# A down projection in split fp32r instead of plain fp32, in a kernel of a recurrent block and a gated FFN

## The chip, the core and the metric

The kernel runs on one core of a Trainium2 chip. A core has a matrix engine (TensorE, PE here; PEld is its weight load), a vector engine (VectorE, DVE), a scalar engine (ScalarE, ACT), GpSimd (POOL) and SyncE (SP), which run their own queues of instructions in order and wait for each other on semaphores. The metric is the device time of one launch in microseconds (us), the median of several runs.

## The reference, cut to what matters

```python
def fp4_quant_dequant(x):                 # blocks of 16 along the last dim
    xb = x.reshape(shape[:-1] + (shape[-1] // BLOCK, BLOCK))
    scale = jnp.maximum(jnp.max(jnp.abs(xb), axis=-1, keepdims=True) / 6.0, 1e-12)
    xn = xb / scale
    return (_GRID[jnp.searchsorted(_MID, jnp.abs(xn))] * jnp.sign(xn) * scale).reshape(shape)

def fp4_linear(x, w):
    return jnp.einsum('bsk,nk->bsn', fp4_quant_dequant(x), fp4_quant_dequant(w))

# x: (16, 512, 256); w_gate, w_up: (704, 256); w_down: (256, 704)
xn = _layernorm(x)
s = recurrent_block(xn)                   # rmsnorm, causal conv, pointwise; minGRU; FFN 256-1024-256
h = silu(fp4_linear(xn, w_gate)) * fp4_linear(xn, w_up)
g = silu(fp4_linear(h, w_down))           # the down projection
out = x + s * g
```

## The kernel before

The 16 sequences are 16 chunks of 512 tokens; a chunk is T = 4 tiles of 128 tokens. A prologue loads and quantises the weights; then `body(c)` runs once for each chunk: chunk 0 and chunk 15 stand alone, chunks 1 to 14 are seven rounds of a loop of two bodies. Each engine has its own list, written out by hand, and there is no scheduler: what stands in the list is the order.

**One chunk on PE.** `gate_up(c, t, h)` makes the gate and up products of tile t, half h (352 of 704 columns), in fp32r: both operands are held as a high part and a remainder, and `product` (L811) issues three products, high by high, high by low, low by high. Among the gate_up groups stand `sum_squares` and `spread_scale` (the rms norm), then come `gru`, `ff2` of the chunk before and `ff1`. The quantised hidden rows (`hq`) of tile t are transposed on PE by `hq_transposes` into banks 2 and 3 of `w_ps` (six tiles of 128 columns), ACT copies them into `hq_t` (`hq_columns`, L693), and `down` (L882) multiplies them by `dn`. The down projection of a chunk is spread out: tile 0 stands at the end of its own body (`hq_transposes(c, 0)`, the transposes of `xq`, `down(c, 0)`, then `pointwise(c + 1)`), tiles 1, 2 and 3 stand in the next chunk's body among its gate_up, gru and ff2.

**Plain fp32.** `hq_t` and `dn` are fp32. `down` runs over six tiles of the 704 hidden columns, of which the sixth has only `LAST` = 64 rows. In the trace each such matmul is two records, so a down tile is 12.

```python
for k in range(KI):
    rows = P if k < KI - 1 else LAST
    last = product(bank[:, 0:D], hq_t[0:rows, k, :], dn[0:rows, k, :], k == 0, k == KI - 1)
```

**One chunk on DVE.** DVE does the quantising of the hidden rows (`hidden_scales`, `fp4_ratios`, `fp4_round`, `hidden_values`), the product of silu and up (`hidden(c, t, h)`, L455), the norms (`add_squares`, `clamp_sums`, `scaled`, `scaled_low`), the scan (`recurrence`), the outputs and the front of the next chunk: `front_moments`, `front_rows`, `front_fp4` (quantises the 512 by 256 inputs, L391 writes `xq`), `front_taps` (the convolution, L443 and L446 write `y`, which `pointwise` reads) and `front_fp4_low` (L452 writes `xq_lo`, which `gate_up(c + 1, 0, 0)` waits for). At the end of a body DVE starts on tile 1's rows (`hidden_scales(c, 1)`), and the next body begins with their rounding and with `conv_residual`, which makes `x1`.

**Waits that matter.** `gate_up(c, t, h)` for t over 0 waits until `hidden` has read the bank of two groups before (`hid_ready`); `hidden` waits for ACT's silu, which waits for PE. `hq_transposes` waits for `hq_ready` from DVE. `sum_squares` waits for `sqs_ready`; in the second half of a chunk it hangs on `recurrence` and the squares on ACT.

Of the kernel before, what the change touches and what calls it, by code (L numbers as in the profile page):

```python
# [19 lines left out]
F32 = mybir.dt.float32  # L20
# [37 lines left out]
def mixed_recurrent_kernel(nc, x, columns, pw_t, gru_t, w1_t, w2_t, w_gate, w_up, w_down, identity, out):  # L58
# [15 lines left out]
    with ctx:  # L74
# [6 lines left out]
        def sem(name):  # L81
# [19 lines left out]
        gu_lo = sb("gu_lo", [P, KD, 2 * NI], F32R)  # L101
        dn = sb("dn", [P, KI, D])

# [17 lines left out]
        x1 = sb("x1", [P, KD, L])  # L121
        sq = sb("sq", [P, KD, L])
        sqs = sb("sqs", [P, L])
        ss_row = sb("ss_row", [P, T])
        inv_rms = sb("inv_rms", [P, T])
        xs = sb("xs", [P, KD, L])
        xs_hi = sb("xs_hi", [P, KD, L], F32R)
        xs_lo = sb("xs_lo", [P, KD, L], F32R)
# [9 lines left out]
        hq = sb("hq", [P, 2, KI * P])  # L138
        hq_t = sb("hq_t", [P, KI, P])
        q_amax = sb("q_amax", [P, 64])  # L140
# [24 lines left out]
            sem(n) for n in ("const_loaded", "gu_loaded", "dn_loaded", "pw_loaded", "gru_loaded",  # L165
                             "w1_loaded", "w2_loaded"))
        constants_ready = sem("constants_ready")
        small_ready = sem("small_ready")
        wscaled = sem("wscaled")
# [5 lines left out]
        wqlo_ready = sem("wqlo_ready")  # L175
        dnt_ready = sem("dnt_ready")
        stats_ready = sem("stats_ready")
# [42 lines left out]
        hqt_done = sem("hqt_done")  # L220
        hqt_ready = sem("hqt_ready")
        dn_done = sem("dn_done")
# [11 lines left out]
        def ff1_bank(j):  # L234

            return gu_ps[:, 1 - j // 2 % 2, j % 2, :]

        def weight_places(p, dst):
# [110 lines left out]
        def _(dve):  # L349
# [116 lines left out]
            def hidden_values(c, t, rounded):  # L466
                dve.wait_ge(hqt_done, KD + T * c + t - 1)
                fp4_values(hq[:, t % 2, 0:NI], NBI, rounded).then_inc(hq_ready, 1)

            def add_squares(n):  # L470

                dve.wait_ge(sq_ready, KD * (n + 1))
                V.tensor_tensor(sqs[:], sq[:, 0, :], sq[:, 1, :], ALU.add).then_inc(sqs_ready, 1)
# [26 lines left out]

            def recurrence(c):

                for k in range(KD):
                    dve.wait_ge(sigh_ready, KD * c + k + 1)
                    V.scalar_tensor_tensor(cand[:, k, :], gu_ps[:, k, 1, :], 0.5, cand[:, k, :],
                                           ALU.add, ALU.max).then_inc(cand_ready, 1)
                    dve.wait_ge(cand_ready, KD * c + k + 1)
                    s = steps.mark(V.tensor_tensor(cand[:, k, :], cand[:, k, :], take[:, k, :], ALU.mult))
                    dve.wait_ge(dve_step, s)
                    s = steps.mark(V.tensor_tensor_scan(x2[:, k, :], keep[:, k, :], cand[:, k, :], 0.0,  # L510
                                                        ALU.mult, ALU.add))
                    dve.wait_ge(dve_step, s)
                    V.tensor_tensor(x2[:, k, :], x2[:, k, :], x1[:, k, :], ALU.add).then_inc(x2_ready, 1)

# [40 lines left out]
            def down_weight(e):  # L555

                dve.wait_ge(wqt_done, NFULL + e)
                quantise(dn_rows[:, e, :], hq[:, e, 0:NI], NBI).then_inc(wq_ready, 1)


            prologue_steps = steps.n
# [4 lines left out]
            def body(c, parity, tail, front):  # L566
# [24 lines left out]
                if tail:  # L591
                    ratios = fp4_ratios(hid[:, 3, :], NBI, scales)
                else:
                    down_weight(1)
                scaled(c * 2, x1, w_ps[:, 1, :])
                if tail:
                    dve.wait_ge(dve_step, ratios)
# [5 lines left out]
                if tail:  # L603
                    hidden_values(c - 1, 3, rounded)
                if front:
                    front_moments(c + 1)
                recurrence(c)
                add_squares(c * 2 + 1)
# [15 lines left out]
                if front:  # L624
                    front_fp4(c + 1)
                    front_taps(c + 1)
                ratios = fp4_ratios(hid[:, 1, :], NBI, hidden_scales(c, 1))
# [6 lines left out]
            for t in range(1, T):  # L634
                if t > 1:
                    ratios = fp4_ratios(hid[:, t, :], NBI, hidden_scales(B - 1, t))
                hidden_values(B - 1, t, fp4_round(NBI, ratios))
            for t in range(T):
                dve.wait_ge(g_ready, T * (B - 1) + t + 1)
                output(B - 1, t, gu_ps[:, t // 2, t % 2, :])  # L640
                dve.wait_ge(sg_ready, T * (B - 1) + t + 1)
                if t == 0:
                    dve.wait_ge(xres_ready, B)
                V.tensor_tensor(o[:, t, :], o[:, t, :], x_res[:, 1, t, :], ALU.add).then_inc(last_ready, 1)
# [3 lines left out]
        def _(act):  # L648
# [24 lines left out]
            def squares(n, ready, c, src):  # L673
                for k in range(KD):
                    act.wait_ge(ready, KD * c + k + 1)
                    act.wait_ge(sqs_ready, n)
                    A.activation(sq[:, k, :], src[:, k, :], ACT.Square).then_inc(sq_ready, 1)

# [14 lines left out]
            def hq_columns(c, t):  # L693
                act.wait_ge(hqt_done, KD + T * c + t + 1)
                act.wait_ge(dn_done, T * c + t)
                A.copy(hq_t[:], w_ps[:, 2:4, :].rearrange("p b n -> p (b n)")[:, 0:KI * P]
                       .rearrange("p (k n) -> p k n", n=P)).then_inc(hqt_ready, 1)

# [56 lines left out]
            def down_columns(e):  # L755
                act.wait_ge(hqt_done, e + 1)
                A.copy(dn[:, :, e * P:(e + 1) * P],
                       w_ps[:, 2:4, :].rearrange("p b n -> p (b n)")[:, 0:KI * P]
                       .rearrange("p (k n) -> p k n", n=P)).then_inc(dnt_ready, 1)

# [47 lines left out]
        def _(pe):  # L808
# [73 lines left out]
            def down(c, t, bank=w_ps[:, 2, :]):  # L882
                pe.wait_ge(hqt_ready, T * c + t + 1)
                for k in range(KI):
                    rows = P if k < KI - 1 else LAST
                    last = product(bank[:, 0:D], hq_t[0:rows, k, :], dn[0:rows, k, :], k == 0, k == KI - 1)
                last.then_inc(dn_done, 1)
# [70 lines left out]
            def down_weight(e):  # L958

                pe.wait_ge(wq_ready, NFULL + 2 + e)  # L960
                pe.wait_ge(dnt_ready, e)
                for k in range(KI):
# [4 lines left out]
            def body(c, parity, tail, front):  # L967
# [32 lines left out]
                if tail:  # L1000
                    ff2(c - 1, 2, w_ps[:, 2, :], (g_ready, T * c))
                    ff2(c - 1, 3, w_ps[:, 3, :], (hqt_ready, T * c))
                ff1(c, range(KF // 2))
                if not tail:
                    pe.wait_ge(dnt_ready, KD)
                if front:
# [65 lines left out]
```

## Time and profile before

| | |
|---|---|
| time, median of 3 runs | 1215.48 us (1215.27 to 1216.74) |
| span of the profiled execution | 1213.5 us |
| PE busy | 1150.5 us (95%) |
| PEld busy | 969.2 us (80%) |
| DVE busy | 1006.4 us (83%) |
| ACT busy | 531.6 us (44%) |
| chain that ended last | PE 92%, DVE 6% |
| down matmuls, 768 records in the trace | 191.5 us busy |

Times in the rows are counted from the start of the span. A timeline row gives start, duration, engine, line, operation, what is written from what, the shape, and in brackets the idle time of the engine before it with what ended that. Matmul records overlap, because PE is pipelined: what a matmul costs is the distance from its start to the next one's start, not its own duration. From about 115 us on every chunk repeats the one before after 70.5 us.

### The profile page before, as it was taken

To read this page: it belongs to the slowest core of one execution; us is meant where nothing else is said; L and a number is where in the kernel's file an instruction comes from. 1 tells how busy PE (TensorE), PEld (TensorE's weight loads), DVE (VectorE), ACT (ScalarE), POOL (GpSimd) and SP (SyncE) were. 2 spreads that over 40 slices of the span, in tenths; PEclk is the share of its full clock that TensorE was granted. 3 is DMA by queue.
4 is the path that set the end of the run, shared out by engine and by line. 5 is a ranking of instruction groups with operands and counts; after the bars stand their busy time and mean duration, and the time that the engine had idled before them with its cause. 6 is when DMAs were issued, how large, how long until landed. Compare 5 with 4: busy or idle time off the path is not lost.

```text
span 1213.5 us, 17503 instructions
## 1 busy us (share of the span) xinstructions
PE 1150.5 (95%) x5922; PEld 969.2 (80%) x5922; DVE 1006.4 (83%) x1844; ACT 531.6 (44%) x839; POOL 144.0 (12%) x122
## 2 busy tenths in 40 slices
PE   3276999999999999999999999999999999999998
PEld 2274888888888887888888798888878888887887
DVE  7868788897978889797888989798897979889783
ACT  4134435453444545444454544445454444545441
POOL 3000010100201020020102011020101102010010
PEclk8587999999999999999999999999999999999999
DMA  6000001000000100000010000001000000100000
GB/s 204 0 1 1 18 1 35 1 19 17 18 18 0 35 0 19 16 18 18 0 35 0 32 4 17 18 0 35 0 35 0 18 18 0 35 0 18 1 18 18
DMA packets 20883, 22.42 MB, mean 18 GB/s; under 512 B 864, under 2 KB 20064, under 8 KB 20832
## 3 DMA queue, kind: packets, MB, share of 16 engines
q1 hardware_dynamic: 20000, 21.04, 5.2%
q10 hardware_dynamic: 832, 0.87, 0.2%
q14 instruction: 39, 0.32, 0.1%
q8 instruction: 12, 0.20, 0.1%
HBM read 13.51 MB, written 8.39 MB: 18 GB/s over the span
## 4 chain that ended last, share of the span: by engine, by line
PE 92%; DVE 6%; issue 0%; ACT 0%; DMA 0%; POOL 0%; ACTq 0%; DVEq 0%; POOLq 0%
PE gu_ps L818 44%; PE w_ps L818 37%; PE w_ps L878 3%; PE w_ps L825 2%; PE gu_ps L861 1%; PE w_ps L924 1%; PE gu_ps L825 1%; PE w_ps L861 1%; DVE q_y L385 1%; DVE q_y L387 1%; DVE q_y L372 1%; DVE q_amax L362 1%; PE gu_ps L870 1%; PE w_ps L870 1%; DVE hq L391 0%
## 5 line engine op out<-in xcount | busy, mean ns | idle before, releaser
L818 PE MATMUL w_ps<-w,act 128*128 128x256 f32 x960 | 217.1, 379 | 0.0
L818 PEld LDWEIGHTS w_ps<-w,act 128*128 128x128 f32 x960 | 177.7, 190 | 21.7
L818 PE MATMUL w_ps<-dn,hq_t 128*128 128x256 f32 (+1 forms) x768 | 191.5, 391 | 0.2
L818 PE MATMUL gu_ps<-gu_hi,xq_hi 128*128 128x352 f32 x512 | 179.0, 350 | 1.0 <-DVE gu_lo L518 1.0
L818 PEld LDWEIGHTS w_ps<-dn,hq_t 128*128 128x128 f32 (+1 forms) x768 | 137.5, 189 | 39.2 <-issue 21.2
L818 PE MATMUL gu_ps<-gu_lo,xq_hi 128*128 128x352 f32 x512 | 167.4, 327 | 0.0
L818 PE MATMUL gu_ps<-gu_hi,xq_lo 128*128 128x352 f32 x512 | 166.6, 325 | 0.0
L458 DVE TENSOR_TENSOR hid<-sl,gu_ps 128x352 f32<-128x352 f32 x128 | 65.6, 513 | 108.0 <-ACT sl L685 107.9
L685 ACT ACTIVATE sl<-gu_ps 128x352 f32<-128x352 f32 x128 | 59.4, 464 | 194.2 <-PE gu_ps L818 193.6
L322 POOL TENSOR_TENSOR inv_rms<-ss_row,neg_half 128x4 f32<-128x4 f32 x32 | 40.5, 1267 | 594.2 <-DVE ss_row L478 594.2
L818 PE MATMUL gu_ps<-xs_hi,w_hi 128*128 128x512 f32 x256 | 106.2, 415 | 4.1 <-DVE xs_lo L491 4.1
L724 ACT ACTIVATE act<-gu_ps,cols 128x512 f32<-128x512 f32 x128 | 86.6, 689 | 53.3 <-PE gu_ps L818 53.1
L818 PEld LDWEIGHTS gu_ps<-gu_hi,xq_hi 128*128 128x128 f32 x512 | 97.7, 191 | 15.0 <-issue 8.6
L818 PE MATMUL gu_ps<-xs_hi,w_lo 128*128 128x512 f32 x256 | 102.8, 401 | 0.0
L818 PE MATMUL gu_ps<-xs_lo,w_hi 128*128 128x512 f32 x256 | 102.3, 400 | 0.0
L818 PEld LDWEIGHTS gu_ps<-gu_lo,xq_hi 128*128 128x128 f32 x512 | 97.8, 191 | 3.6 <-issue 3.6
L818 PEld LDWEIGHTS gu_ps<-gu_hi,xq_lo 128*128 128x128 f32 x512 | 97.5, 190 | 0.0
L691 ACT CAST xs_hi<-xs 128x512 fp32r<-128x512 f32 x64 | 37.8, 617 | 108.7 <-DVE xs L485 108.7
L385 DVE TENSOR_TENSOR q_y<-q_y,q_m 128x704 f32<-128x704 f32 (+3 forms) x88 | 82.4, 937 | 3.0
L387 DVE TENSOR_TENSOR q_y<-q_y,q_m 128x704 f32<-128x704 f32 (+3 forms) x88 | 82.4, 936 | 3.0
L703 ACT ACTIVATE g<-w_ps 128x256 f32<-128x256 f32 x64 | 24.6, 384 | 100.1 <-PE w_ps L818 99.9
L391 DVE TENSOR_TENSOR hq<-q_y,q_scale 128x704 f32<-128x704 f32 (+1 forms) x72 | 62.6, 869 | 1.9
(112 smaller groups left out, 2045.8 us busy)
## 6 DMA issues: line engine op xcount, KB each, us to landing
x_in<-x_dram SPq DMA_DIRECT2D x16, 512.0 KB, 3.5
out_dram<-o SPq DMA_DIRECT2D x15, 512.0 KB, 2.9
act<-w_t_dram SPq DMA_DIRECT2D x1, 1024.0 KB, 11.4
w<-w_t_dram SPq DMA_DIRECT2D x1, 1024.0 KB, 13.9
act<-w_down_dram SPq DMA_DIRECT2D x1, 704.0 KB, 9.5
hid<-w_gate_dram SPq DMA_DIRECT2D x1, 640.0 KB, 5.6
hid<-w_up_dram SPq DMA_DIRECT2D x1, 640.0 KB, 8.7
keep<-gru_t_dram ACTq DMA_DIRECT2D x1, 512.0 KB, 8.0
```

Of the source, the lines that this page charges most:

```text
L322: nc.gpsimd.tensor_tensor(inv_rms[:], ss_row[:], neg_half[:], ALU.pow).then_inc(inv_ready, 1)
L385: s = steps.mark(V.tensor_tensor(yv, yv, mv, ALU.add))
L387: return steps.mark(V.tensor_tensor(yv, yv, mv, ALU.subtract))
L391: return V.tensor_tensor(blocks(dst, nb), blocks(q_y[:, 0:nb * FP4_BLOCK], nb), spread(q_scale[:, 0:nb], nb), ALU.mult)
L458: V.tensor_tensor(hid[:, t, h * HALF:(h + 1) * HALF], sl[:, h, :], gu_ps[:, h, 1, 0:HALF], ALU.mult).then_inc(hid_ready, 1)
L685: A.activation(sl[:, h, :], gu_ps[:, h, 0, 0:HALF], ACT.Silu).then_inc(silu_ready, 1)
L691: A.copy(xs_hi[:, k, :], xs[:, k, :]).then_inc(xshi_ready, 1)
L703: A.activation(g[:, t, :], bank[:, 0:D], ACT.Silu).then_inc(g_ready, 1)
L724: A.activation(act1[:, j, :], ff1_bank(j), ACT.Gelu, bias=b1c[:, j:j + 1]).then_inc(gelu_ready, 1)
L818: done = M.matmul(psum, l, r, start=first and i == 0, stop=last and i == len(terms) - 1)
L825: last = M.transpose(bank[:, t * P:(t + 1) * P], src[:, t, k * P:(k + 1) * P], ident[:])
L878: last = M.transpose(w_ps[:, 2 + k // 4, k % 4 * P:(k % 4 + 1) * P], hq[:, t % 2, k * P:(k + 1) * P], ident[:])
```

## The change

- `dn` becomes `dn_hi` and `dn_lo`, `hq_t` becomes `hqt_hi` and `hqt_lo`, all fp32r. ACT's copy writes the high part; a new DVE instruction subtracts it from what stands in PSUM and writes the remainder: `hidden_low` for the rows, `down_weight_low` for the two halves of the weights, in chunk 0.
- `down` waits for both parts and issues three fp32r products for each of six full tiles (the last 64 columns of `hq` are zero): 18 matmuls instead of six fp32 ones.
- `hidden_low(c - 1, t)` for t = 1, 2, 3 and `hidden_low(c, 0)` are put into DVE's list; `recurrence` is cut into its two halves so that `hidden_low(c - 1, 3)` stands between them.
- `sq`, the buffer of the squares, becomes the same memory as `xs`, with a wait for `xslo_ready` ahead of the squares.

The diff, cut:

```diff
+        sq = xs
...
+            def hidden_low(c, t):
+
+                dve.wait_ge(hqthi_ready, T * c + t + 1)
+                dve.wait_ge(dn_done, T * c + t)
+                V.tensor_tensor(hqt_lo[:], hqt_ps, hqt_hi[:].bitcast(F32), ALU.subtract).then_inc(hqtlo_ready, 1)
...
                 add_squares(c * 2)
+                if tail:
+                    hidden_low(c - 1, 1)
                 hidden(c, 1, 1)
...
+                    down_weight_low(0)
                     down_weight(1)
                 scaled(c * 2, x1, w_ps[:, 1, :])
+                if tail:
+                    hidden_low(c - 1, 2)
...
-                recurrence(c)
+                recurrence(c, 0)
+                if tail:
+                    hidden_low(c - 1, 3)
+                recurrence(c, 1)
...
                 if front:
                     front_fp4(c + 1)
+                hidden_low(c, 0)
+                if front:
                     front_taps(c + 1)
...
                 hidden_values(B - 1, t, fp4_round(NBI, ratios))
+                hidden_low(B - 1, t)
...
                     act.wait_ge(sqs_ready, n)
+                    act.wait_ge(xslo_ready, KD * n)
...
-                A.copy(hq_t[:], w_ps[:, 2:4, :].rearrange("p b n -> p (b n)")[:, 0:KI * P]
-                       .rearrange("p (k n) -> p k n", n=P)).then_inc(hqt_ready, 1)
+                A.copy(hqt_hi[:], hqt_ps).then_inc(hqthi_ready, 1)
...
-                pe.wait_ge(hqt_ready, T * c + t + 1)
+                pe.wait_ge(hqthi_ready, T * c + t + 1)
+                pe.wait_ge(hqtlo_ready, T * c + t + 1)
                 for k in range(KI):
-                    rows = P if k < KI - 1 else LAST
-                    last = product(bank[:, 0:D], hq_t[0:rows, k, :], dn[0:rows, k, :], k == 0, k == KI - 1)
+                    last = product(bank[:, 0:D], (hqt_hi[:, k, :], hqt_lo[:, k, :]),
+                                   (dn_hi[:, k, :], dn_lo[:, k, :]), k == 0, k == KI - 1)
```

Where the new instruction stands in DVE's list. First the end of a body, shown for chunk 0, before (`xq` is the last write of `front_fp4`, `y` that of `front_taps`, `q_amax<-hid` begins the scales of tile 1):

```order
L387 TENSOR_TENSOR q_y<-q_y,q_m 128x1024
L391 TENSOR_TENSOR xq<-q_y,q_scale 128x1024
L443 SCALAR_TENSOR_TENSOR y<-w_ps,cols,y 128x511
L446 SCALAR_TENSOR_TENSOR y<-w_ps,cols,y 128x510
L443 SCALAR_TENSOR_TENSOR y<-w_ps,cols,y 128x511
L446 SCALAR_TENSOR_TENSOR y<-w_ps,cols,y 128x510
L362 TENSOR_REDUCE q_amax<-hid 128x44
```

The same place on DVE after the change:

```order
L394 TENSOR_TENSOR q_y<-q_y,q_m 128x1024
L398 TENSOR_TENSOR xq<-q_y,q_scale 128x1024
L481 TENSOR_TENSOR hqt_lo<-w_ps,hqt_hi 128x768
L450 SCALAR_TENSOR_TENSOR y<-w_ps,cols,y 128x511
L453 SCALAR_TENSOR_TENSOR y<-w_ps,cols,y 128x510
L450 SCALAR_TENSOR_TENSOR y<-w_ps,cols,y 128x511
L453 SCALAR_TENSOR_TENSOR y<-w_ps,cols,y 128x510
L369 TENSOR_REDUCE q_amax<-hid 128x44
```

The remainder of tile 0 now stands ahead of the four instructions of the convolution; all behind it keeps its order. Second, DVE's list around `scaled` in the first half of a body, before (`xs` from `w_ps` is `scaled`, the first `hid` is `hidden(c, 2, 1)`, the second `hidden(c, 3, 0)`):

```order
L458 TENSOR_TENSOR hid<-sl,gu_ps 128x352
L372 TENSOR_TENSOR q_y<-hid,q_inv 128x704
L485 TENSOR_TENSOR xs<-w_ps,x 128x512 x2
L458 TENSOR_TENSOR hid<-sl,gu_ps 128x352
L491 TENSOR_TENSOR xs_lo<-xs,xs_hi 128x512 x2
```

The same place after:

```order
L465 TENSOR_TENSOR hid<-sl,gu_ps 128x352
L379 TENSOR_TENSOR q_y<-hid,q_inv 128x704
L498 TENSOR_TENSOR xs<-w_ps,x 128x512 x2
L481 TENSOR_TENSOR hqt_lo<-w_ps,hqt_hi 128x768
L465 TENSOR_TENSOR hid<-sl,gu_ps 128x352
L504 TENSOR_TENSOR xs_lo<-xs,xs_hi 128x512 x2
```

The remainder of tile 2, for which PE's `down(c - 1, 2)` waits, stands behind `scaled`; nothing else is moved.

## Rows read from the trace of the kernel before

**Rows 1.** The page, busy us, share of the span and instructions of each engine:

```profile
PE 1150.5 (95%) x5922; PEld 969.2 (80%) x5922; DVE 1006.4 (83%) x1844; ACT 531.6 (44%) x839; POOL 144.0 (12%) x122
```

**Rows 2.** Windows, one chunk: length, busy us of PE, PEld, DVE, ACT, POOL, clock, DMA:

```profile
620.12:690.62 70.50, 70.48 (x368) 59.55 (x368) 60.00 (x110) 32.39 (x52) 8.82 (x7) 1.00 0.05 15
```

**Rows 3.** Timeline of PE in that chunk: gate_up(c,1,0), down of tiles 1 and 2, sum_squares:

```profile
631.08 0.40 PE L818 MATMUL gu_ps<-gu_hi,xq_hi 128*128 128x352 f32 x1
...
635.88 3.03 PE L818 MATMUL w_ps<-dn,hq_t 128*128 128x256 f32 x12
638.84 0.43 PE L818 MATMUL gu_ps<-gu_hi,xq_hi 128*128 128x352 f32 x1
...
645.83 2.95 PE L818 MATMUL w_ps<-dn,hq_t 128*128 128x256 f32 x12
...
663.54 1.05 PE L861 MATMUL gu_ps<-ones,sqs 128*128 128x1 f32 x8
```

**Rows 4.** Timeline of PE: 3rd and 24th product of an ff1 and a gate_up group:

```profile
613.28 0.40 PE L818 MATMUL gu_ps<-xs_hi,w_lo 128*128 128x512 f32 x1
...
618.19 0.39 PE L818 MATMUL gu_ps<-xs_hi,w_lo 128*128 128x512 f32 x1
...
626.97 0.32 PE L818 MATMUL gu_ps<-gu_hi,xq_lo 128*128 128x352 f32 x1
...
630.35 0.32 PE L818 MATMUL gu_ps<-gu_hi,xq_lo 128*128 128x352 f32 x1
```

**Rows 5.** Groups of instructions by line and shape, whole span: count, busy us, mean ns:

```profile
L458 DVE TENSOR_TENSOR hid<-sl,gu_ps 128x352 f32<-128x352 f32 x128 | 65.6, 513 | 108.0 <-ACT sl L685 107.9
...
L452 DVE TENSOR_TENSOR xq_lo<-gu_ps,xq_hi 128x512 fp32r<-128x512 f32 x32 | 20.5, 683 | 0.1
```

**Rows 6.** Timeline of DVE: hidden(c,1,1), scaled, hidden(c,3,0), second half of recurrence:

```profile
635.72 0.52 DVE L458 TENSOR_TENSOR hid<-sl,gu_ps 128x352 f32<-128x352 f32 x1 [0.82 <-ACT sl L685]
...
645.46 1.28 DVE L485 TENSOR_TENSOR xs<-w_ps,x 128x512 f32<-128x512 f32 x2
647.78 0.52 DVE L458 TENSOR_TENSOR hid<-sl,gu_ps 128x352 f32<-128x352 f32 x1 [1.05 <-ACT sl L685]
...
658.64 0.68 DVE L505 SCALAR_TENSOR_TENSOR cand<-gu_ps,cand 128x512 f32<-128x512 f32 x1
```

**Rows 7.** Timeline of ACT: the copies of tiles 2, 3 and 0:

```profile
644.10 0.80 ACT L696 COPY hq_t<-w_ps 128x768 f32<-128x768 f32 x1 [0.62 <-PE w_ps L878]
...
657.19 0.80 ACT L696 COPY hq_t<-w_ps 128x768 f32<-128x768 f32 x1
...
689.77 0.80 ACT L696 COPY hq_t<-w_ps 128x768 f32<-128x768 f32 x1
```

**Rows 8.** Timeline of DVE: conv_residual, hidden(c,0,0) of this chunk; first of front_taps:

```profile
625.92 0.75 DVE L498 SCALAR_TENSOR_TENSOR x<-w_ps,cols,xn_t 128x512 f32<-128x512 f32 x1
...
629.34 0.52 DVE L458 TENSOR_TENSOR hid<-sl,gu_ps 128x352 f32<-128x352 f32 x1 [1.75 <-ACT sl L685]
...
686.34 0.74 DVE L443 SCALAR_TENSOR_TENSOR y<-w_ps,cols,y 128x511 f32<-128x511 f32 x1
```

**Rows 9.** Timelines of DVE and ACT in chunk 0, the quantising of w_down:

```profile
76.72 0.88 DVE L362 TENSOR_REDUCE q_amax<-act 128x44 f32<-128x704 f32 x1
...
82.85 1.28 DVE L485 TENSOR_TENSOR xs<-w_ps,x 128x512 f32<-128x512 f32 x2
...
78.99 0.80 ACT L757 COPY dn<-w_ps 128x768 f32<-128x768 f32 x1 [5.01 <-PE w_ps L963]
```

**Rows 10.** PE's wait in chunk 0 (timeline), and the window behind it:

```profile
87.00 0.47 PE L818 MATMUL gu_ps<-xs_hi,gru_hi 128*128 128x512 f32 x1 [2.50 <-DVE xs_lo L491]
...
88.00:91.30 3.30, 3.30 (x9) 2.54 (x8) 1.27 (x9) 1.09 (x2) 1.64 (x4) 0.50 0.00 0
```

**Rows 11.** Timelines at the end: ACT's copy of tile 0, PE's last down:

```profile
1181.51 0.80 ACT L696 COPY hq_t<-w_ps 128x768 f32<-128x768 f32 x1
...
1207.12 2.95 PE L818 MATMUL w_ps<-dn,hq_t 128*128 128x256 f32 x12
```

More of the change, by code:

```diff
@@ L101, in mixed_recurrent_kernel @@
         gu_lo = sb("gu_lo", [P, KD, 2 * NI], F32R)
-        dn = sb("dn", [P, KI, D])
+        dn_hi = sb("dn_hi", [P, KI, D], F32R)
+        dn_lo = sb("dn_lo", [P, KI, D], F32R)
         x_in = sb("x_in", [P, T, D])
@@ L121, in mixed_recurrent_kernel @@
         x1 = sb("x1", [P, KD, L])
-        sq = sb("sq", [P, KD, L])
         sqs = sb("sqs", [P, L])
@@ L138, in mixed_recurrent_kernel @@
         hq = sb("hq", [P, 2, KI * P])
-        hq_t = sb("hq_t", [P, KI, P])
+        hqt_hi = sb("hqt_hi", [P, KI, P], F32R)
+        hqt_lo = sb("hqt_lo", [P, KI, P], F32R)
         q_amax = sb("q_amax", [P, 64])
@@ L166, in mixed_recurrent_kernel @@
                              "w1_loaded", "w2_loaded"))
+        small_ready = sem("small_ready")
         constants_ready = sem("constants_ready")
-        small_ready = sem("small_ready")
         wscaled = sem("wscaled")
@@ L175, in mixed_recurrent_kernel @@
         wqlo_ready = sem("wqlo_ready")
-        dnt_ready = sem("dnt_ready")
+        dnhi_ready = sem("dnhi_ready")
+        dnlo_ready = sem("dnlo_ready")
         stats_ready = sem("stats_ready")
@@ L220, in mixed_recurrent_kernel @@
         hqt_done = sem("hqt_done")
-        hqt_ready = sem("hqt_ready")
+        hqthi_ready = sem("hqthi_ready")
+        hqtlo_ready = sem("hqtlo_ready")
         dn_done = sem("dn_done")
@@ L236, in ff1_bank @@
             return gu_ps[:, 1 - j // 2 % 2, j % 2, :]
+        hqt_ps = (w_ps[:, 2:4, :].rearrange("p b n -> p (b n)")[:, 0:KI * P]
+                  .rearrange("p (k n) -> p k n", n=P))
         def weight_places(p, dst):
@@ L499, in conv_residual, with recurrence @@
                                            ALU.add, ALU.add).then_inc(x1_ready, 1)
[L501 to L513, printed above, removed]
+            def recurrence(c, k):
+                dve.wait_ge(sigh_ready, KD * c + k + 1)
+                V.scalar_tensor_tensor(cand[:, k, :], gu_ps[:, k, 1, :], 0.5, cand[:, k, :],
+                                       ALU.add, ALU.max).then_inc(cand_ready, 1)
+                dve.wait_ge(cand_ready, KD * c + k + 1)
+                s = steps.mark(V.tensor_tensor(cand[:, k, :], cand[:, k, :], take[:, k, :], ALU.mult))
+                dve.wait_ge(dve_step, s)
+                s = steps.mark(V.tensor_tensor_scan(x2[:, k, :], keep[:, k, :], cand[:, k, :], 0.0,
+                                                    ALU.mult, ALU.add))
+                dve.wait_ge(dve_step, s)
+                V.tensor_tensor(x2[:, k, :], x2[:, k, :], x1[:, k, :], ALU.add).then_inc(x2_ready, 1)
             def weight_low(p):
@@ L558, in down_weight, with down_weight_low @@
                 quantise(dn_rows[:, e, :], hq[:, e, 0:NI], NBI).then_inc(wq_ready, 1)
+            def down_weight_low(e):
+                dve.wait_ge(dnhi_ready, e + 1)
+                cut = slice(e * P, (e + 1) * P)
+                V.tensor_tensor(dn_lo[:, :, cut], hqt_ps, dn_hi[:, :, cut].bitcast(F32),
+                                ALU.subtract).then_inc(dnlo_ready, 1)
             prologue_steps = steps.n
@@ L604, in body @@
                     hidden_values(c - 1, 3, rounded)
+                else:
+                    down_weight_low(1)
                 if front:
                     front_moments(c + 1)
-                recurrence(c)
+                recurrence(c, 0)
+                if tail:
+                    hidden_low(c - 1, 3)
+                recurrence(c, 1)
                 add_squares(c * 2 + 1)
@@ L756, in down_columns @@
                 act.wait_ge(hqt_done, e + 1)
-                A.copy(dn[:, :, e * P:(e + 1) * P],
-                       w_ps[:, 2:4, :].rearrange("p b n -> p (b n)")[:, 0:KI * P]
-                       .rearrange("p (k n) -> p k n", n=P)).then_inc(dnt_ready, 1)
+                A.copy(dn_hi[:, :, e * P:(e + 1) * P], hqt_ps).then_inc(dnhi_ready, 1)
             def body(c, parity, tail, front):
@@ L960, in down_weight @@
                 pe.wait_ge(wq_ready, NFULL + 2 + e)
-                pe.wait_ge(dnt_ready, e)
+                pe.wait_ge(dnlo_ready, e)
                 for k in range(KI):
@@ L1001, in body @@
                     ff2(c - 1, 2, w_ps[:, 2, :], (g_ready, T * c))
-                    ff2(c - 1, 3, w_ps[:, 3, :], (hqt_ready, T * c))
+                    ff2(c - 1, 3, w_ps[:, 3, :], (hqtlo_ready, T * c))
                 ff1(c, range(KF // 2))
                 if not tail:
-                    pe.wait_ge(dnt_ready, KD)
+                    pe.wait_ge(dnlo_ready, KD)
                 if front:
@@ L1025, in _ @@
             for t in range(1, T):
-                hq_transposes(B - 1, t, (hqt_ready, T * (B - 1) + t))
+                hq_transposes(B - 1, t, (hqtlo_ready, T * (B - 1) + t))
                 ff2(B - 1, t, gu_ps[:, t // 2, t % 2, :], None)
```

## The prediction

> **What bounds the kernel now.** I read the busy shares first: PE is busy 95% of the span, DVE 83% [rows 1]. Then one steady chunk by windows: from one down product of tile 0 to the next it takes 70.50 us, PE is busy for 70.48 of them at a granted clock of 1.00 (the 2.4 GHz level), DVE for 60.0 [rows 2]. So PE never waits in the loop, DVE has 10.5 us to spare, and a cheaper PE would be worth its saving if nothing took its place. Shares don't say that; places do. So I read, in order of time, where each of DVE's four new instructions (below: A for tile 1, B for tile 2, C for tile 3, D for tile 0) would stand: what DVE does there, when ACT's copy has ended, when PE wants the down product [rows 3, 6, 7, 8]. DVE works its queue in order, so an instruction that waits holds all behind it.
>
> **The price of the product.** Before, a down tile takes 638.84 - 635.88 = 2.96 us [rows 3]. After it is 18 products of 256 columns. The trace has fp32r products of 352 columns every (630.35 - 626.97)/21 = 0.161 us and of 512 columns every (618.19 - 613.28)/21 = 0.234 us [rows 4]: 0.456 ns a column either way. At that rate 256 columns take 0.117; a line with a fixed part, 512/2.4 and 352/2.4 taken off, gives up to 0.125; pure columns at 2.4 GHz 0.107. I take 0.117 (the two rows agree on it), so 18 x 0.117 = 2.10 us, **0.86 us less** per tile, and keep 0.107 to 0.125 for the range. The Trainium skill (TensorE: Matmul & The Clock Gate, Back-to-back issue gap) gives columns/2.4 + 2.5 ns, 109 ns here, and so 1.97 us a tile; by it 352 columns would take 149 ns where the row has 161, so the row decides. By the page the sum below would be some 4 us lower.
>
> **The price of the low part.** DVE's subtraction of 768 columns, one operand in PSUM, is not in the trace; its nearest rows are 352 columns in 513 ns and 512 columns, fp32r out, in 683 ns [rows 5]. Along that line 768 take 955 ns, and the next instruction starts some 0.87 after it. Bounds 0.90 and 1.00. It needs ACT's copy, 0.80 us [rows 7], which I leave as it is. Four of them are 3.8 us a chunk: less than DVE's spare 10.5 us, so the place of each decides. Now the walk, in times of the trace, through one chunk of the changed kernel. I add 0.04 to 0.1 us for a signal from engine to engine, as the rows show it.
>
> *A.* DVE stood idle for 0.82 us before hidden(c,1,1) at 635.72 [rows 6]; A fits in there (634.83 to 635.78), and PE wants the product at 635.88 [rows 3]. Nothing is lost, and all that follows comes 0.86 earlier.
>
> *B.* It stands behind scaled(), which began at 645.46 [rows 6], now 644.60, and lasts 1.20. So B runs from 645.8 to 646.76; ACT's copy (644.10 + 0.80 - 0.86 = 644.04) is long done [rows 7]. PE wants the product at 645.83 - 0.86 = 644.97 [rows 3] and gets it at 646.84: **a stall of 1.9 us**. It ends at 648.94, where the row puts 645.83 + 2.87 = 648.70: 0.24 late instead of 1.7 early. hidden(c,3,0) keeps its -0.86, since B lies in the 1.05 us for which DVE waited there [rows 6].
>
> *C.* Moved 0.24 by PE, ACT's copy runs 657.43 to 658.23 [rows 7]; DVE would be free at about 658.2. C takes 658.28 to 659.23, and recurrence(c,1), at 658.64 before [rows 6], starts at 659.15, 0.51 later. Squares, their sum and PE's sum_squares hang on it: 663.54 [rows 3] becomes 664.04. PE, done with its product at 663.0, stalls 1.0 us. Up to here a chunk has **lost 0.5**, not gained 3.
>
> *D.* From sum_squares to the transposes of tile 0 PE has no down product; that stretch is only moved by 0.5. ACT's copy runs 690.27 to 691.07 [rows 7]. DVE is done with front_fp4 where front_taps began, 686.34 + 0.5 [rows 8], and now stands for **4.2 us**, with front_taps, the scales of tile 1, xq_lo, the rounding of tile 1 and conv_residual queued behind the wait. D runs 691.10 to 692.05 and front_taps starts at 691.97, 5.6 later than before. From front_taps to conv_residual the rows have 625.92 - (686.34 - 70.5) = 10.08 us without a gap [rows 8], then 1.34 for its two instructions: hidden(c+1,0,0) starts at 691.97 + 10.08 + 1.34 = 703.39, not at 629.34 + 70.5 = 699.84, where DVE had waited 1.75 for it [rows 8]. On PE, down D starts at 692.13 and ends at 694.23; pointwise waits for y until 695.0; gate_up(0,0) for xq_lo until 698.6; then gate_up(1,0) for hidden(0,0), until 703.39 + 0.52 + 0.08 = 703.99. Before it began at 631.08 + 0.08 (the last transpose still ran) + 70.5 = 701.66 [rows 3]. **So a chunk takes 2.33 us more**, 72.8 instead of 70.5: 0.5 in its first half, 1.8 in the second. From there ACT and DVE again wait for PE (DVE by 0.8 us), so the next chunk begins in the same phase and the loss repeats.
>
> The rest of the edits. sq sharing xs makes the squares wait for xs_lo, which DVE made more than 10 us earlier (after 647.78, against 658.64 [rows 6]): nothing; without that cover it would cost the squares' start. The zero rows of the sixth tile are in the 18 products already.
>
> **Ends.** In chunk 0 down_weight_low(0) stands where the quantising of the second half of w_down began, 76.72 [rows 9], and needs ACT's copy, 78.99 + 0.80 [rows 9]; so that begins at 80.7, and as DVE is then the engine waited for (PE idle 2.50 at 87.00 [rows 10]), +4.0. D of chunk 0 adds 1.8. In the last chunk the first half adds 0.5; then D holds the quantising of tiles 1 to 3, done before under ff1, until ACT's copy, 1181.51 + 0.5 + 0.80 [rows 11]. It starts at 1183.7; each tile then goes round in quantising (82.85 - 76.72 = 6.1 to 6.3, from chunk 0 [rows 9]), transposes and copy 1.8, low part 0.9: 9.0. The last down product starts at 1183.7 + 6.3 + 2 x 9.0 + 4.4 (transposes and ff2 ahead of it) = 1212.4, not 1207.12 [rows 11], and is 0.86 shorter: +4.4 with the 0.5.
>
> **Sum.** 14 chunk periods x 2.33 = 32.6; chunk 0: 4.0 + 1.8; end: 4.4; together **+42.8 us**. The profiled span is 1213.5, the median 1215.48, 2.0 above it: 1213.5 + 42.8 + 2.0 = **1258 us**, 3.5% slower. Bounds: 36 products on the path of a chunk (down A and B) at 0.107 to 0.125, -5 to +4; three low parts at 0.90 to 1.00, 2 either way; ten signals by 0.05 each, 7 either way; chunk 0 and the end -2 to +7, mostly for the clock. As the price of this case: 1245 to 1275.
>
> **Rivals.**
> *Faster: the low parts vanish in DVE's spare time and PE alone decides.* For it: 70.48 of 70.50 us and DVE's 10.5 [rows 2]. Then 64 tiles x 0.86 = 55 us come off: 1160. It decides at D: ACT's copy would have to end by 686.3 for DVE to run through; it ends 4 us later, behind ff1. Between this and the forecast lies no change, if some 2.3 us of D's wait cost nothing: 1213 to 1218.
> *The clock falls.* In this trace PE stood idle for 2.50 us at 87.00, and 88.0 to 91.3 was granted 0.50, the 1.2 GHz level [rows 10]; the loop, without idle time, had 1.00 [rows 2]. My stalls are 1.9, 1.0, 1.0, 0.8, 0.2 and 0.8 us. If one a chunk took the clock down for such a stretch, PE would lose some 1.7 of 3.3 us: 14 x 1.7 = 24, so 1282, and twice that for two. It decides between idle times of 1.9 and 2.5 us. The Trainium skill (TensorE: Matmul & The Clock Gate, A second HAM failure mode: psum-queue depth-cycling) tells of a kernel in which brief idling of PE between groups of matmuls makes the clock swing between its two levels; by that rule this is the case to fear.
> *It doesn't do what it says: an fp32r product of 256 columns is no cheaper than half a plain fp32 one.* Then 18 x 0.216 (2.96 us less the half tile's edges, by 12) = 3.9 a tile; A and B carry 1.8 more each, 14 x 3.6 = 50: about 1310. Against it, the even 0.456 ns of 352 and 512 columns.
>
> **How the numbers follow.** Forecast 0.79, faster 0.07, no change 0.04, clock 0.06, no cheaper product 0.04. The forecast's own range, 1245 to 1275, holds perhaps nine tenths of its case; 1236 to 1290 takes in nearly all of it and half of the clock's: eight in ten. Within 0.2% (2.4 us, about what a measurement of this kernel can tell from no change) is 0.04; faster 0.07; slower 0.89.
>
> **What would show it.** In the profile after: down tiles of about 2.1 us; PE idle some 5.7 us a chunk, by the names of the low part (at B), sqs, y, xq_lo and hid; DVE idle before each low part of tile 0 for about 4.2 us, on ACT's copy; a period near 72.8; quantising strung out behind ff1 at the end. Wrong would be: no DVE wait at D (then the rivals hold), a half clock inside the loop, or products far from 0.117 us.

## The result, and the profile after

The changed kernel takes **1282.0 us** (median of 4 runs, 1280.8 to 1282.7) against 1216.1 of the kernel before, run beside it (1215.3 to 1217.5): a ratio of 1.055, 95% interval 1.053 to 1.056. Slower, as forecast, and inside the wide range (1236 to 1290), but 24 us above the point of 1258 and outside the forecast's own range (1245 to 1275). The profiled span is 1280.5 us, 67.0 above that of before. Three lines of its page: busy time, the queue q8, which brings blocks of instructions (packets, MB, share), and the chain that ended last:

```profile
PE 1126.8 (88%) x6306; PEld 980.0 (77%) x6306; DVE 1060.8 (83%) x1910; ACT 531.8 (42%) x839; POOL 144.1 (11%) x122
...
q8 instruction: 67, 1.10, 0.4%
...
PE 58%; DVE 29%; issue 8%; ACT 4%; DVEq 1%; DMA 0%; POOL 0%; ACTq 0%; POOLq 0%
```

PE does 24 us less than in [rows 1] and is no longer the only bound: a chain that was 92% PE is now 58%, with DVE at 29% and 8% "issue", which is an engine that waits for nothing the profile shows. The prices, from the groups of the whole span:

```profile
L848 PE MATMUL w_ps<-dn_hi,hqt_hi 128*128 128x256 f32 x384 | 114.9, 299 | 42.9 <-DVE hqt_lo L481 42.9
...
L481 DVE TENSOR_TENSOR hqt_lo<-w_ps,hqt_hi 128x768 fp32r<-128x768 f32 x64 | 61.0, 953 | 80.3 <-ACT hqt_hi L729 80.3
...
L729 ACT CAST hqt_hi<-w_ps 128x768 fp32r<-128x768 f32 x64 | 51.2, 800 | 31.1 <-PE w_ps L908 30.3
```

The low part takes 953 ns on DVE (955 were worked out), ACT's copy 800 as in [rows 7]. Now PE at the places of the walk, in one chunk: pointwise, gate_up(c,1,0), the first product of tile 1, the tile of tile 2 (first, second and last product), sum_squares, and the first product of tile 0 (D):

```profile
804.93 3.70 PE L848 MATMUL w_ps<-y,pw 128*128 128x512 f32 x8 [0.41 <-DVE y L453]
...
813.88 0.43 PE L848 MATMUL gu_ps<-gu_hi,xq_hi 128*128 128x352 f32 x1 [0.54 <-DVE hid L465]
...
818.74 0.36 PE L848 MATMUL w_ps<-dn_hi,hqt_hi 128*128 128x256 f32 x1
...
829.75 0.35 PE L848 MATMUL w_ps<-dn_hi,hqt_hi 128*128 128x256 f32 x1 [1.76 <-DVE hqt_lo L481]
829.94 0.28 PE L848 MATMUL w_ps<-dn_lo,hqt_hi 128*128 128x256 f32 x1
...
831.85 0.28 PE L848 MATMUL w_ps<-dn_hi,hqt_lo 128*128 128x256 f32 x1
...
846.89 1.05 PE L891 MATMUL gu_ps<-ones,sqs 128*128 128x1 f32 x8 [0.79 <-DVE sqs L486]
...
875.05 0.36 PE L848 MATMUL w_ps<-dn_hi,hqt_hi 128*128 128x256 f32 x1 [1.10 <-DVE hqt_lo L481]
```

From the second product to the 18th it is 1.91 / 16 = 0.119 us each; 0.117 was taken. The first of a tile costs 0.19, so a tile is 2.2 us where 2.10 was forecast. PE's waits stand where the walk put them: 1.76 at B, 0.79 before sum_squares, 0.41 for y, 0.54 for hid, and 1.10 at D; tile 1 (A) has none. DVE, first at the end of an even chunk and then at the end of the odd one behind it (remainder of tile 0, first rounding of tile 1, conv_residual):

```profile
725.82 0.96 DVE L481 TENSOR_TENSOR hqt_lo<-w_ps,hqt_hi 128x768 fp32r<-128x768 f32 x1 [4.18 <-ACT hqt_hi L729]
...
735.47 0.53 DVE L388 TENSOR_SCALAR q_e<-q_y 128x704 uint16<-128x704 uint16 x1 [2.21 <-issue]
...
739.07 1.40 DVE L511 SCALAR_TENSOR_TENSOR x<-w_ps,cols,xn_t 128x512 f32<-128x512 f32 x2
...
801.04 0.96 DVE L481 TENSOR_TENSOR hqt_lo<-w_ps,hqt_hi 128x768 fp32r<-128x768 f32 x1 [4.19 <-ACT hqt_hi L729]
...
808.40 0.52 DVE L388 TENSOR_SCALAR q_e<-q_y 128x704 uint16<-128x704 uint16 x1
...
812.00 1.40 DVE L511 SCALAR_TENSOR_TENSOR x<-w_ps,cols,xn_t 128x512 f32<-128x512 f32 x2
```

D is as forecast in both: 4.2 us on ACT's copy, with the same work queued behind. But from the low part to conv_residual it is 739.07 - 725.82 = 13.25 us in the first and 812.00 - 801.04 = 10.96 in the second; the 2.29 between them are DVE's 2.21 of "issue". The first is the return from the loop's second body to its head. There are six returns, 14.7 us on DVE by the list of waits, and the ACT copy of tile 0 stands 11.78 us ahead of conv_residual without one and 14.1 to 14.6 with one. Periods (from sum_squares to sum_squares) of chunks without a return or a clock fall are 72.85 to 72.9; 72.8 was forecast. With a return they are 75.2 and more. And there is a clock fall: windows of PE, before and during one (length, busy PE, PEld, DVE, ACT, POOL, clock, DMA):

```profile
885.30:888.64 3.34, 1.42 (x10) 0.89 (x8) 3.27 (x6) 0.60 (x2) 0.00 (x0) 1.00 0.00 0
888.64:892.05 3.41, 2.86 (x10) 2.86 (x11) 2.37 (x7) 1.71 (x3) 0.00 (x0) 0.50 0.02 5
```

That one stands behind a return. The loop had five such stretches of 3.41 us at 1.2 GHz, four behind a return and one behind the stall at B; each made its chunk 1.3 to 1.6 us longer. **The balance:** forecast 42.8 + six returns 15.3 + five clock falls 7.3 = 65.4, of 67.0 measured.

### The profile page after: what moved, and what is told of

Its sections match the earlier page's. It is cut to its first block, busy times and chain, and to the rows that moved or that the text cites. A ratio compares the mean times of both kernels' runs of the same rounds, so it can differ in the third digit from the quotient of the medians.

```text
span 1280.5 us, 18484 instructions
## 1 busy us (share of the span) xinstructions
PE 1126.8 (88%) x6306; PEld 980.0 (77%) x6306; DVE 1060.8 (83%) x1910; ACT 531.8 (42%) x839; POOL 144.1 (11%) x122
## 4 chain that ended last, share of the span: by engine, by line
PE 58%; DVE 29%; issue 8%; ACT 4%; DVEq 1%; DMA 0%; POOL 0%; ACTq 0%; POOLq 0%
PE gu_ps L848 32%; PE w_ps L848 18%; DVE q_amax L369 3%; DVE hqt_lo L481 3%; ACT hqt_hi L729 2%; PE w_ps L855 2%; PE w_ps L908 2%; DVE y L450 2%; DVE q_y L392 2%; DVE q_y L394 2%; DVE hq L398 2%; DVE x L522 2%; DVE x L511 2%; PE gu_ps L891 1%; DVE xq_lo L459 1%
## 5 line engine op out<-in xcount | busy, mean ns | idle before, releaser
L848 PE MATMUL gu_ps<-gu_hi,xq_hi 128*128 128x352 f32 x512 | 174.1, 340 | 13.9 <-DVE hid L465 9.5
L848 PE MATMUL w_ps<-dn_hi,hqt_hi 128*128 128x256 f32 x384 | 114.9, 299 | 42.9 <-DVE hqt_lo L481 42.9
L481 DVE TENSOR_TENSOR hqt_lo<-w_ps,hqt_hi 128x768 fp32r<-128x768 f32 x64 | 61.0, 953 | 80.3 <-ACT hqt_hi L729 80.3
L848 PEld LDWEIGHTS w_ps<-dn_hi,hqt_hi 128*128 128x128 f32 x384 | 72.6, 189 | 50.3 <-issue 49.8
L848 PE MATMUL w_ps<-dn_hi,hqt_lo 128*128 128x256 f32 x384 | 108.2, 282 | 0.0
L848 PE MATMUL w_ps<-dn_lo,hqt_hi 128*128 128x256 f32 x384 | 108.0, 281 | 0.0
```

Of the source, the lines that this page charges most:

```text
L481: V.tensor_tensor(hqt_lo[:], hqt_ps, hqt_hi[:].bitcast(F32), ALU.subtract).then_inc(hqtlo_ready, 1)
L848: done = M.matmul(psum, l, r, start=first and i == 0, stop=last and i == len(terms) - 1)
```

## The experiments

All ratios are against the kernel before, run on the same chip beside each.

**1. The return, and whose.** In the kernel before the return was there too, on DVE, and PE ran on:

```profile
553.67 0.53 DVE L381 TENSOR_SCALAR q_e<-q_y 128x704 uint16<-128x704 uint16 x1 [1.75 <-issue]
```

Three runs write out one engine's list for all chunks and leave the rest:

```diff
-            ratios = over_chunks(dve, body)
+            ratios = over_chunks(dve, body, True)   # for c in range(1, B - 1): body(...)
```

> The changed kernel, with VectorE's list written out for all 16 chunks instead of a loop of two bodies; the other engines keep their loops. The profile after shows every second chunk 2.3 to 4.4 us longer than the 72.85 of the others, and DVE idle for 2.2 to 2.7 us at its return to the loop's head, with nothing to wait for. Theory DVE: that return, which lay beside a wait of 1.75 us before the change, is now on the path, since the low part of tile 0 took the slack, and the half clock that follows it is its result; without it all periods are near 72.9 and the time is 1282 less 15.3 (six returns) less 7.3 (five stretches of half clock): about 1260, 1258 to 1268. Rival PE: PE's own return (1.66 us idle, its weight load 2.48) and its instruction blocks, 67 fetched instead of 12, set the pace; then this run stays within 4 us of 1282. Rival neither (something else goes by twos, such as the two halves of x_res): also 1282.

Measured: 1268.9 us (1266.4 to 1270.2), 13 less, 0.9 above what was expected at most. DVE has no idle time at the former returns, and every chunk has 11.85 us from copy to conv_residual: the returns were on the path, worth their 15.3. But the clock did not recover with them. There are again four stretches at 1.2 GHz in the loop, all behind the stall at B. One of them, the stall on PE's timeline and the window behind it:

```profile
305.48 0.36 PE L852 MATMUL w_ps<-dn_hi,hqt_hi 128*128 128x256 f32 x1 [1.76 <-DVE hqt_lo L485]
```

```profile
306.42:309.83 3.41, 3.41 (x17) 3.41 (x16) 3.31 (x6) 0.38 (x1) 0.00 (x0) 0.50 0.02 5
```

So half of the theory fell: with the returns gone, the stalls of the change bring the half clock by themselves. That doesn't clear the returns: in the change four of five such stretches stood behind one, in the next run six of six. (Periods without one are 73.0, 0.15 longer than with the loop; why, stayed open.)

> The changed kernel, with TensorE's list written out for all 16 chunks; VectorE and the rest keep their loops. Theory DVE: PE waits at that place for hidden(c,0,0), which hangs on DVE's return to the loop's head, so PE's own return lies beside it; 1275 to 1282, the periods still alternate. If the fetches of PE slow those of DVE, DVE's wait falls from 2.4 to the 1.8 us that it was before the change, 4 us less. Rival PE: about 1260, periods even at 72.9.

Measured: 1290.6 us (1287.5 to 1293.6), 8.5 slower than the change and outside both forecasts. PE's own return is gone and buys nothing, which speaks for the theory DVE, though its number (1275 to 1282) missed. DVE's returns grew instead to 2.9 us on average (17.6 in all), and a clock fall came behind each of the six. That DVE's return depends on PE's list at all was not expected, in this direction least, and stays open; in four_places below it doesn't (0.9 to 1.1 us with PE's loop, 1.0 without).

> The kernel before, with VectorE's list written out for all 16 chunks; the control for the return to the loop's head. Theory of the cover: before the change that return (1.75 to 1.9 us on DVE) lay beside a wait of 1.75 us for hidden(c,0,0) and PE ran on, so taking it away brings nothing: 1213 to 1217, up to 1218 if a written-out list costs 0.2 us a chunk as it did in the changed kernel. Rival, a return always costs its 1.8 us: 6 x 1.8 = 11 us less, 1204.

Measured: 1214.9 us, ratio 1.000 (0.999 to 1.001); the periods stay 70.50. Together with the first run this is the point missed: the same idle time, 1.8 us on DVE, cost nothing while DVE had 1.75 to wait for hidden(c,0,0) [rows 8], and all of it once D had eaten that wait. What DVE does at a return can be told from another queue of instruction blocks, here in the kernel before and then in this run:

```profile
q14 instruction: 39, 0.32, 0.1%
```

```profile
q14 instruction: 19, 0.16, 0.0%
```

It goes from 40 to 20 in dve_unrolled too and stays at 39 in pe_unrolled, so it seems to be DVE's own: DVE's loop is read again in each round, and in the trace of the kernel before a read starts 1.0 to 1.3 us behind each taken branch, inside or just ahead of the idle time.

**2. Place D.**

```diff
                 if front:
                     front_fp4(c + 1)
-                hidden_low(c, 0)
-                if front:
                     front_taps(c + 1)
+                hidden_low(c, 0)
```

> The changed kernel with one instruction moved: the remainder of the rows of tile 0 stands behind the four instructions of the convolution instead of ahead of them; all loops stay. Theory of place D: of DVE's wait of 4.2 us for ACT's copy some 1.3 are left, since 2.9 us of work now stand ahead of it; y is ready early; the period falls from 72.85 to about 71.1, and the return to the loop's head costs some 0.9 instead of 2.5: 1213.5 + 14 x 0.56 + 6 x 0.9 + 4.0 (chunk 0) + 5.3 (end) + 2 = 1238, to 1245 if the half clock still comes behind the returns. Rival: the loss lies in the low parts' own time on DVE and the waits of PE at the other three tiles, not in the place of this one; then less than 10 us come off, 1272 or more.

Measured: 1240.9 us (1239.6 to 1242.2), ratio 1.021 (1.018 to 1.023): 41 less than the change, for one instruction moved by four. The period is 71.25, and 71.2 to 71.5 with a return, so the returns are covered again. DVE's wait for the copy is what was left over:

```profile
918.80 0.96 DVE L481 TENSOR_TENSOR hqt_lo<-w_ps,hqt_hi 128x768 fp32r<-128x768 f32 x1 [1.30 <-ACT hqt_hi L728]
```

**3. The low parts taken away, the product kept.** `hidden_low` does nothing, its buffer is zero and PE waits for `hqthi_ready` alone.

> The changed kernel without the remainder of the hidden rows: DVE's four subtractions a chunk are left out, their buffer is zero, and PE's three products for each of six tiles are all kept and wait for ACT's copy alone. So DVE has before's work, and PE the new product. Theory (the product is 0.86 us cheaper a tile, but only the savings ahead of hidden(c,1,1) and at the end of a chunk reach the path, since the squares of the second half hang on DVE's recurrence): period 68.4 to 68.9, with 0.9 more at each return to the loop's head; 1188 to 1200. Rival, PE alone decides: all four savings count, period 67.1, about 1165. Rival, the new product is no cheaper on the path: 1213 or more.

Measured: 1196.1 us (1195.1 to 1198.0), ratio 0.984; periods 68.75, every third 70.4 with a clock fall. So the product itself brings some 20 us (the interval of the ratio is 0.982 to 0.987), and making and waiting for the low parts of the rows costs 86, the returns that this uncovers among them. Even without them the second half hangs on the recurrence: PE waits 1.28 before sum_squares there, so "PE alone decides" (1165) fails for this order.

**4. One stall of PE taken away: B alone.**

```diff
                 hidden(c, 2, 1)
                 if tail:
-                    ratios = fp4_ratios(hid[:, 3, :], NBI, scales)
+                    hidden_low(c - 1, 2)
...
                 scaled(c * 2, x1, w_ps[:, 1, :])
                 if tail:
-                    hidden_low(c - 1, 2)
+                    ratios = fp4_ratios(hid[:, 3, :], NBI, scales)
...
+                silu_gate(c, 3, (0,))
                 high_part(c * 2, (ff1_done, KF * c))
-                silu_gate(c, 3, (0,))
```

The last part is ScalarE's list.

> The changed kernel with the remainder of tile 2 moved ahead of scaled() on VectorE (the ratios of tile 3 behind it), and on ScalarE the silu of hidden(c,3,0) ahead of the high part of xs, so that PE gets its down product of tile 2 without the stall of 1.9 us. Theory chain: between hidden(c,2,1) and recurrence(c,0) DVE is idle for only some 0.6 us, so the recurrence and with it sum_squares come 0.4 to 0.6 us earlier and no more; PE's wait before sum_squares grows from 0.8 to about 2.2 in exchange; 1272 to 1277. Rival, each stall of PE counts for itself: the period falls by 1.8, 14 x 1.8 = 25, and the half clocks that follow this stall go too: 1249 to 1257.

Measured: 1287.6 us (1287.3 to 1295.4), 5.6 *slower* than the change. The period without a fall is 72.6, 0.26 shorter, as the chain theory has it; the stall of 1.76 moved to sum_squares, where it is now 2.1 (36.1 us in all, 17.7 in the change). What neither theory had is the clock. Sum_squares on PE's timeline, and the window behind it:

```profile
399.17 1.05 PE L890 MATMUL gu_ps<-ones,sqs 128*128 128x1 f32 x8 [2.09 <-DVE sqs L486]
```

```profile
401.38:404.79 3.41, 3.41 (x9) 2.71 (x9) 2.94 (x10) 0.00 (x0) 0.40 (x1) 0.50 0.02 5
```

In this profile (the run of 1295) eleven of the loop's 14 chunks lose 1.7 to 3.3 us right behind that wait, and two lose some 2.5 more behind a return. The other four runs, 1287 to 1289, were granted a mean clock of 0.960 to 0.961 against 0.955, so they must have had fewer such stretches. One stall of 2.1 us in place of stalls of 1.76 and 0.79 cost more than the idle time that it saved.

**5. All four places.** If places are the cause, other places must give the 86 us back.

```diff
                 recurrence(c, 0)
+                recurrence(c, 1)
                 if tail:
                     hidden_low(c - 1, 3)
-                recurrence(c, 1)
                 add_squares(c * 2 + 1)
...
                     ff2(c - 1, 0, w_ps[:, 0, :], (ss_ready, 2 * c + 1))
-                    down(c - 1, 3)
+                    ff2(c - 1, 1, w_ps[:, 1, :], (xs_ready, KD * (2 * c + 1)))
                 sum_squares(c * 2 + 1, gu_ps[:, 0, 0, :], (coef_ready, KD * c + 1))
                 if tail:
-                    ff2(c - 1, 1, w_ps[:, 1, :], (xs_ready, KD * (2 * c + 1)))
+                    down(c - 1, 3)
...
-                down(c, 0, w_ps[:, 2 if front else 0, :])
                 if front:
                     pointwise(c + 1)
+                down(c, 0, w_ps[:, 2 if front else 0, :])
```

with the edits of 2 and 4; `hidden_scales(c, 0)` ahead of `clamp_sums`, `down_weight_low(0)` behind `down_weight(1)`, and the last chunk's low parts each behind a later rounding.

> The changed kernel with all four remainders at other places: tile 0 behind the convolution, and PE's pointwise ahead of its down product; tile 2 ahead of scaled(); tile 3 behind the whole recurrence, with PE taking ff2 of tile 1 and sum_squares first and the down product of tile 3 after them; in chunk 0 the remainder of the first half of w_down behind the quantising of the second; at the end each remainder behind the rounding of a later tile. Theory of places: with no wait of PE for a remainder the period is what PE has to do, 68.4 to 69.8 us (67.6 busy of 71.3 in the run with tile 0 moved), so 1213.5 - 14 x 1.4 + 1 + 2 + 2 = 1199, 1190 to 1207, faster than before. Rival, DVE's 3.8 us more a chunk cannot be hidden anywhere, since its chain of squares, scan and norms sets the second half: 1225 to 1240, near the run with tile 0 moved alone.

Measured: **1182.2 us** (1179.7 to 1185.2), ratio 0.972 (0.970 to 0.973): 100 us under the change, 33 under the kernel before, with the same instructions, and below the range expected, since the period fell to 67.7 and not only to 68.4. It is 14 more than the 86 asked for: PE's wait before sum_squares, still 1.28 in run 3, is gone too, as PE takes ff2 first. So the moves of PE's own steps have a share that no run here separates; the kernel before had no wait in its loop that they could take away [rows 2]. Periods are 67.7, except where a return lies: there 69.6 to 69.7, and 71.2 to 71.4 at three of the six, which a stretch at 1.2 GHz follows (the profile is of the run of 1185.2). The page's line for the blocks of instructions reads as in the change (67), and PE's list of waits has (us in all, times, longest):

```profile
PE gu_ps L850 <- issue: 11.2, 6, 2.0
```

> The run four_places with VectorE's list also written out. If the returns are still covered there, it is the same or up to 3 us slower (0.2 us a chunk, as in the changed kernel); if they are on the path, 6 to 12 us faster than four_places.

Measured: 1181.3 us (1181.0 to 1182.2): DVE's returns are covered. Now it is PE's own return that is left, 10.6 us in this run.

**6. PE's return.** The kernel before shows no such gap on PE, and its page reads "q8 instruction: 12, 0.20, 0.1%". The change's 18 matmuls a tile instead of six made PE's loop longer: in the trace of the kernel before q8 reads no block between 248 and 1120 us, in the change nine in each further round.

```diff
-                body(i * 2 + 1, 1, True, True)
-                body(i * 2 + 2, 0, True, True)
+            with engine.Fori(0, B - 2) as i:   # TensorE alone
+                body(i + 1, 1, True, True)
```

> The run four_places with TensorE's loop of seven rounds of two chunks made 14 rounds of one chunk; the others keep theirs. In four_places PE stands idle for 1.9 us at each of its six returns to the loop's head with nothing to wait for, and its instruction queue moves 67 blocks of 16 KB; the kernel before moves 12 and runs on without a gap. Theory of fetches: a loop of one chunk is half as long and stays where it is once read, so the blocks fall to 20 or fewer, no return shows a gap, every period is near 67.8: 1182 - 11 = 1171, 1168 to 1175. Rival, a return costs PE 1.9 us whatever the loop's length: 13 returns instead of six, 1195.

Measured: 1175.4 us (1175.2 to 1175.6), just above the range expected, since every second period is still 68.8 to 69.0. Thirteen returns, none with a gap on PE. The page's line for the blocks, and from PE's list of waits what is left at the six returns of DVE's loop:

```profile
q8 instruction: 9, 0.15, 0.1%
```

```profile
PE gu_ps L854 <- DVE hid L469: 4.8, 6, 0.8
```

> The run four_places with TensorE's list written out for all chunks: no return at all. Theory of fetches: the blocks are read in order, ahead of use, so some 50 of them cost nothing: 1168 to 1175. Rival, it is not the return but something else that comes at every second chunk (the stores, GpSimd's sum, VectorE's own return): 1182.

Measured: 1175.1 us (1173.9 to 1176.1), 51 blocks, no gap. Both agree with the theory of fetches in place and in blocks; the gain is 7 instead of 11, because DVE's return, 1.0 us, is next. A part of the 7 is the clock: three falls behind PE's returns in the profile of four_places, none in these two.

Blocks read again are not yet a gap, though. The run no_row_remainder moves 67 blocks too, and PE runs on at all six returns; here the first, pointwise and the gate_up behind it, and then the last return of four_places:

```profile
269.46 3.60 PE L847 MATMUL w_ps<-y,pw 128*128 128x512 f32 x8
272.50 0.72 PE L847 MATMUL gu_ps<-gu_hi,xq_hi 128*128 128x352 f32 x1
```

```profile
957.45 0.42 PE L850 MATMUL gu_ps<-gu_hi,xq_hi 128*128 128x352 f32 x1 [1.95 <-issue]
```

In both traces that gate_up starts about 4 us behind PE's branch (4.1 to 4.2, and 3.9 to 4.2). In no_row_remainder PE still has 4.7 us of products queued when its list branches, pointwise last; in four_places, where pointwise was moved ahead of the down tile, it has 2.2 us. So the move that freed place D uncovered PE's return; no run puts pointwise back to test it by itself. Nor does the loop's length alone decide: low0_behind_taps has the change's list on PE, reads 31 blocks (again in only two of the six further rounds) and shows no gap; why stayed open.

> The run four_places_pe_short_loop with VectorE's list written out as well. There DVE stands idle for 1.1 us at each of six returns, PE waits up to 0.8 for hidden(c,0,0) behind them and every second period is 68.9 instead of 67.75. Theory: these 1.1 are now the only return on the path; 1175.4 - 6 x 1.1 = 1169, 1167 to 1171, all periods 67.75. Rival, something else that comes at every second chunk is late there: 1175.

Measured: **1167.1 us** (1165.7 to 1168.2), ratio 0.959 (0.958 to 0.961). All 14 periods after chunk 0's are 67.70 to 67.76, with no clock fall in the loop. One of them, as a window:

```profile
617.00:684.75 67.75, 67.62 (x394) 59.60 (x393) 63.02 (x114) 32.53 (x51) 8.78 (x7) 1.00 0.05 16
```

PE is busy for 67.62 of 67.75 us, as it was for 70.48 of 70.50 in [rows 2]. The rival of the prediction, that PE alone decides (1160), is nearly what the same change does with other places and no returns.

## Why the prediction was right in sign and 24 us short

- **Prices.** Right: 0.119 for the product (0.117), 953 ns for the low part (955). A tile is 2.2 instead of 2.10, because the first product of a tile costs 0.19; that is two tiles on the path, about 0.2 us a chunk. (The line with a fixed part gives up to 0.127, not 0.125. Nothing hung on it. The formula quoted from the Trainium skill (TensorE: Matmul & The Clock Gate, Back-to-back issue gap) is stated there for an isolated matmul, not for a stream of them; it gives 0.109 where 0.119 was measured.)
- **A to D.** Right in each place but one small one (0.2 for xq_lo, which PE didn't wait for): the waits were 1.76 (1.9 forecast) at B, 0.79 (1.0) at C, 1.10 (1.0) and 0.41 (0.8) at D, 0.54 (0.8) for hid, DVE's 4.18 (4.2). The period came out at 72.85 to 72.9 (72.8). That the sum agrees is luck in part, by one chunk (length, busy PE, PEld, DVE, ACT, POOL, clock, DMA):

```profile
804.93:877.85 72.92, 68.33 (x393) 59.75 (x393) 63.31 (x114) 32.40 (x53) 8.81 (x7) 1.00 0.05 16
```

  PE stood idle for 4.6 us instead of 5.7, but was busy for 68.3 where the walk's prices make 70.48 - 4 x 0.86 = 67.0; the two misses cancel. Run 2 shows D's share: 41 us, of which 15 x 1.6 = 24 are the period (72.85 to 71.25); most of the rest are the returns, which the slack that is left covers again.
- **Ends.** Right: up to gate_up(1,0) of chunk 1 +5.5 (5.8 forecast), the end +5.3 (4.4).
- **14 periods alike: the step that failed first.** The walk took "in times of the trace" one chunk, in which DVE comes to the next body without a return, and multiplied it by 14. Six of the 14 have 2.3 to 2.9 us more. The row for it stood in the trace before (553.67 above), with PE running on; the walk has no term for it, and itself spent its cover, the 1.75 us, at D. Term missed: 15.3 us.
- **The clock: a rival's price, in part.** The forecast took it for one case of 0.06 in which each chunk pays, and put the threshold between 1.9 and 2.5 us. Stalls of 1.76 were followed by a fall in one of 14 chunks in the change, in none in pe_unrolled and in four of 14 in dve_unrolled; four of the change's six returns had one, where PE stood idle for 0.1 to 1.9 us several times in a row. It was neither nothing nor every chunk: 7.3 us. The Trainium skill (TensorE: Matmul & The Clock Gate, A second HAM failure mode: psum-queue depth-cycling) has the direction right: idling of 1.8 us between groups of matmuls was enough, though in four of 14 chunks at most.
- **That it came to 1282**, the very number of the clock rival, is no support for it: that rival had 24 us of clock and no returns; there were 7 and 15.

## What to carry to other kernels

When a change spends an engine's slack, list everything that this slack had covered, the loop's return among it: look at one chunk with a return and one without, on every engine, before multiplying. A new step between two engines is paid by its place, not by its length: the same change cost 66 us with its new instructions at one set of places and gave 33 at another (49 without returns). And a stall taken away in one place may only gather in the next, as a step moved from one place may uncover what it covered there; one long wait can cost more than two short ones, if it takes the clock down.

## What was not expected of the hardware

- **PE's loop can be read again in every round.** In the kernel before it was read once (12 blocks of 16 KB in all), in the change again in each round after (67). In four_places each return then left PE idle for 1.7 to 2.0 us. Half as long a loop: 9 blocks, no gap. The list written out: 51 blocks, no gap. Where PE still had 4.7 us to do, reading again left no gap (no_row_remainder), and the same list can be read again at some returns and not at others (low0_behind_taps). The Trainium skill (Runtime: NRT & Kernel Launch, Instruction fetch mechanics) says that a taken branch whose target is no longer held makes the engine fetch it before it goes on, and that PE holds more than most. The runs agree: in four_places a block's read starts 0.9 to 1.2 us behind PE's branch and the returns leave 11.2 us idle in all; and q14, if it is DVE's, shows DVE's loop read again in each round where PE's still was not (39 blocks against 12 in the kernel before).
- **DVE's returns** left DVE idle for 0.9 to 3.1 us, at each return of each run that keeps DVE's loop, also in the kernel before (10.8 us in all, six times, covered there). They were longest in pe_unrolled.
- **A clock fall in the loop** lasted 3.41 us and cost 1.3 to 1.7, but for three of 6.83 in low2_ahead_scaled. Stalls of 2.1 us brought one in 11 of 14 chunks, stalls of 1.28 (no_row_remainder) in four of 14, of 1.76 in none to four of 14, PE's returns of 1.5 to 2.0 in one (four_places_dve_unrolled) and three (four_places) of six, and stalls of 0.8 to 1.1 alone in none.
